# A graph layer on one core: hand-fetched sender rows in every third round instead of every sixth

## The chip, the cores and the metric

The kernel runs on one core of a Trainium2 chip. The metric is device microseconds of one execution, the median of the runs shown. A profile of one execution shows the five engines: PE (TensorE, with its weight loads as PEld), DVE (VectorE), ACT (ScalarE), POOL (GpSimd) and SP (SyncE, which here only starts transfers). Rows named SPq, ACTq and POOLq are instructions that the engine's queue handles itself, such as starting a transfer.

## The reference

One layer of message passing over 12,500 nodes with 128 features and 200,000 edges, sorted by receiver, all in float32:

```python
h = jnp.maximum(_layernorm(x), 0.0)
cat = jnp.concatenate((h[src], h[dst], edge_attr), axis=-1)      # 200000 x 384
msg = jax.nn.relu(cat @ W1 + b1)                                 # 200000 x 128
aggr = jax.ops.segment_sum(msg, dst, num_segments=12500)
t = aggr + h
x = x + gamma * (t - mean(t)) * rsqrt(var(t) + eps) + beta
```

## The kernel before

W1 is split in three. `table_a = h @ W1[0:128]` and `table_b = h @ W1[128:256] + b1` are built per node in DRAM. A message is then a row of `table_a` taken by sender, a row of `table_b` taken by receiver, and the edge's features times the last third of W1.

A **group** is 512 edges: 128 partitions by SUB = 4 edges. There are 391 groups (the last overlaps the one before), UNROLL = 4 of them make a **round**, and there are 98 rounds. Below, (i, u) is group u of round i.

For each group, PE transposes the edge features (`ps_edge`, L756), and ACT copies them out (`edge_cols`, `columns`, L991). DVE writes a one-hot matrix that picks receivers out of a window of 64 rows of `table_b` (`onehot_cols`, `hot_columns`, L1367); SP has loaded that window (`b_win`, `window`, L486) at the group's least receiver, a number that is read into a register. PE makes both products into `ps_pre` (L769, L770). The sender rows come by four gathers on POOL (`a_rows`, L613, in `step`), each an indirect DMA of 128 rows whose numbers DVE wrote a round ahead (`pick`, L1192). DVE adds rows and products (`msg`, `add_a`, L1387), ACT applies the relu (`relu`, L995), PE sums by receiver (`sums`, L781), DVE adds the sums to `aggr` at the group's base (`add_sums`, L1408), which it reads into a register for every group (L1398).

What orders the gathers: `step(i, u)` on POOL waits until `pick` has run for (i, u) and until the add of (i-1, u) has freed `a_rows[:, u]`. So POOL may run four groups ahead of DVE.

Two kinds of work spare POOL gathers. (1) In every sixth round (EARLY = 6), group 3 takes no gather: its `x` rows were gathered at the very start (64 gathers, L588), turned into table rows during the first 64 rounds by a side chain on DVE, PE and ACT (`early_columns` L1007, `keep_early` L1013), stored in `table_early` and loaded by SP in one transfer (`load_early`, L497). (2) In every sixth round (PERIOD = 6) group 0 takes three gathers and not four: the 128 rows of its last quarter are fetched **by hand**, one transfer of 512 bytes per row, 64 rows from SP (`fetch`, L508) and 64 from ACT (`fetch`, L1027). Each fetch loads row numbers from `hand_picks` into registers (L363), 8 at a time on SP, 4 on ACT. SP's are spread over rounds 1 to 4 of the six, ACT's likewise, in the instruction order of their queues. DVE adds the hand rows in an instruction of its own (L1394) behind the add of the other three quarters (L1390).

SP's queue is one list in order. For a round it holds: load four bases; the edges and receivers of groups 0 and 1 (`pair`, L461, L462, which waits for PE and DVE to be done with that half of the round before); windows 0 and 1 (each waits for the products of the same group of the round before, L485); a fetch; the other pair; windows 2 and 3; a fetch; the store of a finished block (L490). The loop on SP and the loop on ACT have a body of six rounds.

ACT's queue in step u of a round: `columns` of the next group; a fetch; in step 3 `deviate` (L973) and `early_columns`; in step 1 `keep_early`; then `relu` of this group.

Of the kernel before, what the change touches and what calls it, by code (L numbers as in the profile page):

```python
# [25 lines left out]
I32 = mybir.dt.int32  # L26
U8 = mybir.dt.uint8
# [4 lines left out]
P = 128  # L32
H = 128
# [14 lines left out]
PERIOD = 6  # L48
BATCH = 8
HAND_K = SUB - 1  # L50
ACT_ROWS = 64
# [7 lines left out]
def build(nc, x, src, dst, edge_attr, w1, b1, gamma, beta, out):  # L59
# [29 lines left out]

    assert HANDS * PERIOD == ROUNDS - 2 and EARLY % PERIOD == 0 and SP_ROWS % BATCH == 0  # L90
    assert PER_GROUP * (UNROLL - 1) + LEAD + WIN <= 3 * P
# [6 lines left out]
    with ctx:  # L98
# [9 lines left out]

        x_all = sb("x_all", [P, ALL_BLOCKS, H])
# [4 lines left out]
        base_i = sb("base_i", [1, ID_ROWS], I32)  # L114
# [13 lines left out]
        flag = sb("flag", [1, 1], I32)  # L128

# [37 lines left out]
        hand_picks = sb("hand_picks", [HANDS, P], I32)  # L167
        hand_rows = sb("hand_rows", [P, 1, H])
# [84 lines left out]
        s_a_rows = [[sem(f"s_a_rows{u}_{k}") for k in range(SUB)] for u in range(UNROLL)]  # L253
# [37 lines left out]
        s_hand_rows = [sem("s_hand_rows")]  # L291
# [12 lines left out]
        s_e_stored = sem("s_e_stored")  # L304
        s_early_loaded = sem("s_early_loaded")
# [43 lines left out]
        def hand_row(p, par):  # L349
            return hand_rows[p:p + 1, par, :].bitcast(U8)  # L350
# [4 lines left out]
        def hand_numbers(t, first, n):  # L355

            if isinstance(t, int):
                return hand_picks[t:t + 1, first:first + n]
            return bass.at_runtime_partition(hand_picks[0:1, first:first + n], t)

        def numbers_of(engine, t, first, n):

            _, numbers = nc.values_load_multi_w_load_instructions(  # L363
                hand_numbers(t, first, n), [engine], min_val=0, max_val=(N - 1) * ROW_BYTES,
                skip_runtime_bounds_check_because="src holds node numbers")
            return numbers
# [14 lines left out]
        def _(sp):  # L381
# [71 lines left out]
            with sp.If(crooked < 1):  # L453
# [18 lines left out]
                def bases(i):  # L472

                    _, values = nc.values_load_multi_w_load_instructions(
                        base_i[0:1, bass.ds(i * UNROLL, UNROLL)], [mybir.EngineType.SP], min_val=0, max_val=N - 1,
                        skip_runtime_bounds_check_because="the least receiver of a group is a node")
                    return values
# [23 lines left out]
                def fetch(t, par, batch):  # L501

                    if batch == 0 and past(t, 1):
                        sp.wait_ge(s_z, ((t - 1) * PERIOD + PERIOD - 1) * UNROLL + 1)
                        sp.sem_inc(s_gate_sp, 1)
                    numbers = numbers_of(mybir.EngineType.SP, t, batch * BATCH, BATCH)
                    for n in range(BATCH):
                        sp.dma_start(hand_row(batch * BATCH + n, par), row_at(numbers[n])  # L508
                                     ).then_inc(s_hand_rows[par], 16)

                def round_(i, t=None, par=None, j=None):
                    base = bases(i)
                    for u in range(UNROLL):
                        if u % PAIR == 0:
                            pair(i, u // PAIR)
                        window(i, u, base[u])
                        if t is not None and (j, u) in SP_SLOTS:
                            fetch(t, par, SP_SLOTS.index((j, u)))
# [3 lines left out]
                def rounds(s):  # L522
                    for j in range(EARLY):
                        n = j // PERIOD
                        round_(s * EARLY + j, s * (EARLY // PERIOD) + n, 0, j % PERIOD)
                    load_early(s)

                SP_SLOTS = [(j, u) for j in range(1, PERIOD - 1) for u in (1, 3)]
                assert len(SP_SLOTS) * BATCH == SP_ROWS
# [5 lines left out]
                rounds(0)  # L535
                with sp.Fori(1, EARLY_GROUPS) as s:
                    rounds(s)
                round_(ROUNDS - 2)
                base = bases(ROUNDS - 1)
                pair(ROUNDS - 1, 0)  # L540
                for u in range(LEFT):
                    if u == PAIR:
                        tail()
                    window(ROUNDS - 1, u, base[u])
# [25 lines left out]
        def _(pool):  # L570
# [35 lines left out]
            with pool.If(crooked < 1):  # L606
                def step(i, u, gathers=SUB):
# [4 lines left out]
                    for k in range(gathers):  # L612
# [3 lines left out]
                        ).then_inc(s_a_rows[u][k], 16)  # L616

                def rounds(s):

                    for n in range(EARLY // PERIOD):  # L620
# [3 lines left out]
                        for u in range(UNROLL if n < EARLY // PERIOD - 1 else UNROLL - 1):  # L624
# [981 lines left out]
```

## Time and profile before

| | us |
|---|---|
| runs shown, lowest to highest | 2840.32 to 2862.66 |
| median of the 3 runs | 2849.47 |
| span of the profiled execution, first to last instruction | 1949.5 |
| median less span: what lies around the instructions | 899.97 |

The profile gives the span of its execution and no device time beside it, so that execution's own time is taken as its span and the 899.97 us that the median has around it. Nothing in the trace shows what these 900 us are. Busy shares are shares of the span; "idle before" is time in which the engine did nothing before an instruction, with what ended the wait. Line numbers are those of the kernel before.

### The profile page before, as it was taken

How to read it: one execution, taken by the hardware profiler on the slowest of the kernel's cores; microseconds unless marked ns; L12 is line 12 of the kernel's file. 1: busy time of each engine (PE TensorE's matmuls, PEld its weight loads, DVE VectorE, ACT ScalarE, POOL GpSimd, SP SyncE). 2: the span in 40 equal slices, each digit the busy share in tenths (PEclk: the TensorE clock that was granted, in tenths of full speed). 3: DMA queues.
4: the chain of work that ended last, by engine and by line, in shares of the span. 5: the costliest groups of instructions: out<-in, count | busy, mean ns of one | idle time of the engine just before them, and what ended most of it. 6: DMA issues, size and time to landing. Idle time of an engine off the chain costs nothing.

```text
span 1949.5 us, 52908 instructions
## 1 busy us (share of the span) xinstructions
PE 1548.5 (79%) x11881; PEld 1483.7 (76%) x11881; DVE 1256.9 (64%) x3454; ACT 659.4 (34%) x1507; POOL 1463.9 (75%) x1559
## 2 busy tenths in 40 slices
PE   5688788778878787877787788787788888877887
PEld 5678788777777777877777787777777877777786
DVE  7656666667666666666666676666566665656665
ACT  5533333333333333333333333333323232322323
POOL 7777777777777777777777777777777777777776
PEclk9888888989889998998989998999898888888988
DMA  9755656556565655656565565656556565555554
GB/s 261 204 143 144 167 143 166 152 156 166 144 169 145 164 152 155 163 147 169 149 160 153 155 166 144 168 140 168 147 154 163 138 164 148 155 148 153 163 145 106
DMA packets 229468, 306.84 MB, mean 157 GB/s; under 512 B 46461, under 2 KB 141157, under 8 KB 229317
## 3 DMA queue, kind: packets, MB, share of 16 engines
q1 hardware_dynamic: 151858, 192.55, 34.4%
q0 software_dynamic: 49536, 101.55, 21.4%
q10 hardware_dynamic: 27922, 11.43, 2.7%
q14 instruction: 143, 1.16, 0.2%
q8 instruction: 9, 0.15, 0.0%
HBM read 281.72 MB, written 23.64 MB: 157 GB/s over the span
## 4 chain that ended last, share of the span: by engine, by line
issue 22%; DMA 22%; POOL 20%; PE 13%; DVE 10%; DVEq 8%; ACT 2%; ACTq 2%; POOLq 1%; SPq 0%
DMA a_rows<-table_a,picks 20%; POOL a_rows L613 19%; DVEq L1398 5%; DVE onehot_cols L1367 3%; PE ps_pre L769 3%; PE ps_pre L770 3%; PE ps_sum L781 2%; DVE msg L1387 2%; PE ps_edge L756 2%; PE ps_fin L781 1%; DVE aggr L1408 1%; ACTq L1027 1%; DMA table_a<-a_out 1%; DVEq L1383 1%; PE ps_sum L788 1%
## 5 line engine op out<-in xcount | busy, mean ns | idle before, releaser
L613 POOL DMA_INDIRECT a_rows<-table_a,picks x1484 | 1401.8, 945 | 452.4 <-issue 400.3
L769 PE MATMUL ps_pre<-w_c,edge_cols 128*128 128x128 f32 x3128 | 671.5, 300 | 29.5 <-issue 29.2
L770 PE MATMUL ps_pre<-b_win,onehot_cols 128*128 128x128 f32 x3128 | 663.2, 297 | 0.0
L995 ACT ACTIVATE msg<-msg 128x512 f32<-128x512 f32 x390 | 245.7, 630 | 951.9 <-DVE msg L1387 893.1
L769 PEld LDWEIGHTS ps_pre<-w_c,edge_cols 128*128 128x128 f32 x3128 | 537.1, 215 | 38.6 <-issue 37.0
L1387 DVE TENSOR_TENSOR msg<-ps_pre,a_rows 128x512 f32<-128x512 f32 x374 | 257.0, 687 | 433.8 <-DMA a_rows<-table_a,picks 339.4
L770 PEld LDWEIGHTS ps_pre<-b_win,onehot_cols 128*128 128x128 f32 x3128 | 534.7, 214 | 0.0
L1367 DVE SCALAR_TENSOR_TENSOR onehot_cols<-space,base_all,ps_hot 64x512 f32<-64x512 int32 x391 | 438.3, 1121 | 0.6 <-DMA space<-in_dst 0.6
L781 PE MATMUL ps_sum<-onehot,msg 128*128 128x64 f32 x1560 | 214.6, 283 | 105.2 <-ACT e_rows L1013 71.3
L781 PEld LDWEIGHTS ps_sum<-onehot,msg 128*128 128x128 f32 x1560 | 200.5, 201 | 123.4 <-ACT e_rows L1013 82.2
L991 ACT ACTIVATE edge_cols<-ps_edge 128x512 f32<-128x512 f32 x391 | 228.4, 584 | 136.8 <-PE ps_edge L756 115.7
L756 PE MATMUL ps_edge<-ident,edges 128*128 128x128 f32 x1564 | 264.9, 297 | 8.4 <-DMA edges<-in_edge_attr 8.4
L781 PE MATMUL ps_fin<-onehot,msg 128*128 128x64 f32 x1560 | 212.2, 283 | 5.6 <-ACT msg L995 5.6
L781 PEld LDWEIGHTS ps_fin<-onehot,msg 128*128 128x128 f32 x1560 | 205.2, 205 | 7.3 <-DVE aggr L1408 6.9
L756 PEld LDWEIGHTS ps_edge<-ident,edges 128*128 128x128 f32 x1564 | 201.6, 162 | 10.5 <-DMA edges<-in_edge_attr 5.9
L1355 DVE TENSOR_TENSOR onehot<-dst_f,ps_hot 128x256 f32<-128x256 f32 x391 | 161.0, 412 | 41.8 <-issue 34.5
L788 PE MATMUL ps_sum<-ident,e_norm 128*128 128x128 f32 x64 | 24.8, 388 | 120.8 <-DVE e_norm L1426 120.8
L788 PEld LDWEIGHTS ps_sum<-ident,e_norm 128*128 128x128 f32 x64 | 10.0, 156 | 129.8 <-DVE e_norm L1426 129.8
L737 PE MATMUL ps_fin<-ident,staged 128*128 128x128 f32 x97 | 29.6, 305 | 79.3 <-DVE aggr L1408 76.0
L1408 DVE TENSOR_TENSOR aggr<-ps_fin,aggr 128x64 f32 x195 | 43.9, 225 | 72.0 <-issue 44.6
L1408 DVE TENSOR_TENSOR aggr<-ps_sum,aggr 128x64 f32 x196 | 43.8, 224 | 65.8 <-PE ps_sum L781 37.9
L737 PEld LDWEIGHTS ps_fin<-ident,staged 128*128 128x128 f32 x97 | 14.4, 149 | 85.4 <-DVE aggr L1408 83.8
(137 smaller groups left out, 1073.8 us busy)
## 6 DMA issues: line engine op xcount, KB each, us to landing
edges<-in_edge_attr SPq DMA_DIRECT2D x195, 512.0 KB
space<-in_dst SPq DMA_DIRECT2D x195, 256.0 KB
a_rows<-table_a,picks POOLq DMA_INDIRECT x1484
hand_rows<-table_a SPq DMA_DIRECT2D x1024, 0.5 KB
hand_rows<-table_a ACTq DMA_DIRECT2D x1024, 0.5 KB
b_win<-table_b SPq DMA_DIRECT2D x391, 32.0 KB
table_b<-b_rows ACTq DMA_DIRECT2D x96, 64.0 KB
out<-out_rows SPq DMA_DIRECT2D x96, 64.0 KB
```

The costliest lines, as they stand in the source:

```text
L613: pool.indirect_dma_start(a_rows[:, u, k, :], None, table_a[:, :], bass.IndirectOffsetOnAxis(ap=picks[:, u, k:k + 1], axis=0),).then_inc(s ...
L756: mm = pe.transpose(ps_edge[u % 2][:, k * P:(k + 1) * P], edges[:, u, k * H:(k + 1) * H], ident[:, :])
L769: pe.matmul(to, edge_cols[:, u % 2, k * P:(k + 1) * P], w_c[:, :], start=True, stop=False)
L770: mm = pe.matmul(to, onehot_cols[:, u % 2, k * P:(k + 1) * P], b_win[:, u, :], start=False, stop=True)
L781: mm = pe.matmul(ps_sums[u % 2], msg[:, u % 2, k, :], onehot[:, u, k, 0:WIN], start=(k == 0), stop=(k == SUB - 1))
L991: act.activation(edge_cols[:, u % 2, :], ps_edge[u % 2][:, :], ACT.Copy).then_inc(s_edge_cols, 1)
L995: act.activation(msg[:, u % 2, :, :], msg[:, u % 2, :, :], ACT.Relu).then_inc(s_msg, 1)
L1355: dve.tensor_tensor(onehot[:, u, :, 0:WIN], dst_f[:, bass.ds(i * UNROLL + u, 1), :].rearrange("p o k -> p (o k)").unsqueeze(2) .to_broadca ...
L1367: dve.scalar_tensor_tensor(out=onehot_cols[0:WIN, u % 2, :].rearrange("w (k p) -> w k p", k=SUB), in0=dst_win[:, u, :].rearrange("w (p k) ...
L1387: dve.tensor_tensor(msg[:, u % 2, :, :].rearrange("p k f -> p (k f)"), ps_pre[u % 2][:, :], a_rows[:, u, :, :].rearrange("p k f -> p (k f) ...
L1398: return dve.value_load(base_i[0:1, bass.ds(g, 1)], min_val=0, max_val=N - 1)
L1408: dve.tensor_tensor(at, ps_sums[u % 2], at, ALU.add).then_inc(s_added, 1)
```

## The change

- PERIOD becomes 3: a quarter of group 0 is fetched by hand in each third round, 32 quarters and no longer 16. POOL does 1468 gathers in the rounds and no longer 1484.
- The split of the 128 rows becomes 72 on SP (nine batches of 8) and 56 on ACT (seven batches of 8, no longer batches of 4). SP has three batches in each round; ACT's lie at steps 0, 2 and 3 of the first two rounds of a period and one at step 2 of the hand round, for the next period.
- `hand_picks` and the bases for SP (`base_sp`) are laid out in places of 16 numbers, so that what one load reads begins on 64 bytes. SP loads 12 bases once for three rounds; DVE loads four once for a round (`base_dve`), and no longer one for each group.
- SP issues the two windows of a half round together, behind one wait for the second group's products; a fetch may lie before the first windows, between windows and pair, between pair and windows, and behind the last windows.
- The loop bodies of SP and ACT hold three rounds; SP's is nested (two of them, then `load_early`), and so are DVE's and POOL's.
- On ACT `early_columns` moves ahead of `columns` in step 3, and the fetch behind `deviate`.
- The four semaphores of the gathers of a group become one; hand rows are waited for by three counts (SP's first five batches, SP's others, ACT's).

```diff
-PERIOD = 6
+PERIOD = 3
 BATCH = 8
+PLACE = 16
-ACT_ROWS = 64
+ACT_ROWS = 56
+FIRST_BATCHES = 5
...
+        def hand_used(t):
+            return ((t - 1) * PERIOD + PERIOD - 1) * UNROLL + 1
...
-                def window(i, u, base):
-                    if u == 0:
+                def windows(i, h, base, end=PAIR):
+                    if h == 0:
                         sp.wait_ge(s_b_stored, 16 if isinstance(i, int) and i < 2 else (i - 1) * 16)
                         sp.sem_inc(s_gate_sp, 1)
                     if past(i, 1):
-                        sp.wait_ge(s_pre, (i - 1) * UNROLL + u + 1)
+                        sp.wait_ge(s_pre, (i - 1) * UNROLL + h * PAIR + end)
                     sp.sem_inc(s_gate_sp, 1)
-                    sp.dma_start(b_win[0:WIN, u, :], table_b[bass.ds(base, WIN), :]).then_inc(s_b_win[u], 16)
+                    for u in range(h * PAIR, h * PAIR + end):
+                        sp.dma_start(b_win[0:WIN, u, :], table_b[bass.ds(base[u], WIN), :]).then_inc(s_b_win[u], 16)
...
+                SLOTS = ((None, 0, 1, 2), (3, 4, 5, None), (6, 7, 8, None))
+                def rounds(t):
+                    base = load_bases(mybir.EngineType.SP, base_sp, t * PLACE, PERIOD * UNROLL)
+                    for j in range(PERIOD):
+                        round_(t * PERIOD + j, base[j * UNROLL:(j + 1) * UNROLL], t, SLOTS[j])
...
+                def round_(i, base, t=None, slots=(None,) * 4):
+                    pair(i, 0)
+                    if slots[0] is not None:
+                        fetch(t, slots[0])
+                    windows(i, 0, base)
+                    if slots[1] is not None:
+                        fetch(t, slots[1])
+                    pair(i, 1)
+                    if slots[2] is not None:
+                        fetch(t, slots[2])
+                    windows(i, 1, base)
+                    if slots[3] is not None:
+                        fetch(t, slots[3])
                     if past(i, 3):
                         store(i - 3)
...
                 with sp.Fori(1, EARLY_GROUPS) as s:
-                    rounds(s)
+                    with sp.Fori(0, 2) as n:
+                        rounds(s * 2 + n)
+                    load_early(s)
...
                     for u in range(groups):
+                        if u == 3 and early:
+                            early_columns(i)
                         if not (last and u == groups - 1):
                             columns(*after(i, u, 1))
-                        if t is not None and j * UNROLL + u < len(ACT_SLOTS) and ACT_SLOTS[j * UNROLL + u]:
-                            fetch(t, par, j * UNROLL + u)
                         if u == 3 and past(i, 2):
                             deviate(i - 2)
-                        if u == 3 and early:
-                            early_columns(i)
+                        for batch in slots[u]:
+                            fetch(t, batch)
...
+                NEXT, SLOTS = ((), (), (0,), ()), (((1,), (), (2,), (3,)), ((4,), (), (5,), (6,)))
...
                 def round_(i, turn, groups=UNROLL, early=False, handed=None, loaded=None):
+                    base = load_bases(mybir.EngineType.DVE, base_dve, i * UNROLL, UNROLL)
...
-                            add_sums(*before(i, u))
+                            add_sums(*before(i, u), base[u])
```

## Rows read from the trace of the kernel before

**Rows 1.** The page: span, and what each engine was busy.

```profile
span 1949.5 us, 52908 instructions
PE 1548.5 (79%) x11881; PEld 1483.7 (76%) x11881; DVE 1256.9 (64%) x3454; ACT 659.4 (34%) x1507; POOL 1463.9 (75%) x1559
```

**Rows 2.** Groups by line on POOL: busy us, mean ns, idle before and its releasers.

```profile
L613 POOL DMA_INDIRECT a_rows<-table_a,picks x1484 | 1401.8, 945 | 452.4 <-issue 400.3 <-DVE picks L1192 52.1
```

**Rows 3.** Waits of POOL: total us, times, longest.

```profile
POOL a_rows L613 <- issue: 400.3, 1313, 0.3
POOL a_rows L613 <- DVE picks L1192: 52.1, 171, 0.3
```

**Rows 4.** Timeline of POOL: the first early gather, the change-over, the last gather.

```profile
5.56 1.10 POOL L588 DMA_INDIRECT aggr<-in_x,early_picks  x1 [3.23 <-DMA early_picks<-in_src]
...
84.39 0.94 POOL L588 DMA_INDIRECT aggr<-in_x,early_picks  x1 [0.30 <-issue]
85.64 0.95 POOL L613 DMA_INDIRECT a_rows<-table_a,picks  x1 [0.30 <-issue]
...
1938.58 0.95 POOL L613 DMA_INDIRECT a_rows<-table_a,picks  x1 [0.30 <-issue]
```

**Rows 5.** Waits of DVE: total us, times, longest.

```profile
DVE msg L1387 <- DMA a_rows<-table_a,picks: 339.4, 154, 5.4
DVE aggr L1408 <- issue: 70.1, 213, 1.2
```

**Rows 6.** Waits of SP's queue: total us, times, longest.

```profile
SPq L485 <- PE ps_pre L770: 350.1, 106, 8.8
SPq L459 <- DVE onehot_cols L1367: 160.7, 73, 8.5
SPq L490 <- DVE out_rows L1340: 87.2, 35, 5.3
```

**Rows 7.** Timeline of SP's queue, one round with two batches and the next one's start.

```profile
799.78 0.41 SPq L461 DMA_DIRECT2D edges<-in_edge_attr  x1
...
801.39 1.26 SPq L486 DMA_DIRECT2D b_win<-table_b  x2
803.38 2.56 SPq L508 DMA_DIRECT2D hand_rows<-table_a  x8
806.21 0.40 SPq L461 DMA_DIRECT2D edges<-in_edge_attr  x1
...
807.64 5.63 SPq L486 DMA_DIRECT2D b_win<-table_b  x2
814.37 2.50 SPq L508 DMA_DIRECT2D hand_rows<-table_a  x8
817.08 0.40 SPq L490 DMA_DIRECT2D out<-out_rows  x1
818.55 0.40 SPq L461 DMA_DIRECT2D edges<-in_edge_attr  x1
```

**Rows 8.** Timeline of SP's queue at the end of its loop's body.

```profile
872.92 0.38 SPq L490 DMA_DIRECT2D out<-out_rows  x1
873.65 0.38 SPq L497 DMA_DIRECT2D a_rows<-table_early  x1
878.00 0.38 SPq L461 DMA_DIRECT2D edges<-in_edge_attr  x1
878.59 0.54 SPq L462 DMA_DIRECT2D space<-in_dst  x1
879.63 1.28 SPq L486 DMA_DIRECT2D b_win<-table_b  x2
881.19 0.39 SPq L461 DMA_DIRECT2D edges<-in_edge_attr  x1
```

**Rows 9.** Timeline of SP's queue and of DVE, the last hand round.

```profile
1880.21 0.41 SPq L461 DMA_DIRECT2D edges<-in_edge_attr  x1
1880.80 0.53 SPq L462 DMA_DIRECT2D space<-in_dst  x1
1881.80 1.27 SPq L486 DMA_DIRECT2D b_win<-table_b  x2
1887.37 0.38 SPq L461 DMA_DIRECT2D edges<-in_edge_attr  x1
...
1896.88 0.54 DVE L1390 TENSOR_TENSOR msg<-ps_pre,a_rows 128x384 f32<-128x384 f32 x1
1897.35 0.27 DVE L1394 TENSOR_TENSOR msg<-ps_pre,hand_rows 128x128 f32<-128x128 f32 x1
```

**Rows 10.** Instructions on the hand rows: ns min/median/max, first and last start.

```profile
L508 SPq DMA_DIRECT2D hand_rows<-table_a x1024: 218/225/328, 93.3 to 1878.0; - x171
L1027 ACTq DMA_DIRECT2D hand_rows<-table_a x1024: 231/235/707, 111.0 to 1891.8; - x171
L1394 DVE TENSOR_TENSOR msg<-ps_pre,hand_rows x16: 268/280/281, 193.1 to 1897.3; 128x128 f32<-128x128 f32 x16
```

**Rows 11.** Timeline of ACT and its queue, step 3 of a round.

```profile
1890.55 1.44 ACTq L1027 DMA_DIRECT2D hand_rows<-table_a  x4
1892.10 0.29 ACT L973 ACTIVATE o_dev<-o_moments,eps 128x1 f32<-128x1 f32 x1 [1.60 <-issue]
1894.18 0.63 ACT L995 ACTIVATE msg<-msg 128x512 f32<-128x512 f32 x1 [1.79 <-DVE msg L1387]
```

**Rows 12.** DMA issues: KB each, us from issue to landing, the shortest two shown.

```profile
table_a<-a_out SPq DMA_DIRECT2D x13, 448.0 KB, 3.9
early_picks<-in_src ACTq DMA_DIRECT2D x1, 4.0 KB, 3.9
```

**Rows 13.** Waits of PE for ACT and for edges: total us, times, longest.

```profile
PE ps_sum L781 <- ACT e_rows L1013: 71.3, 55, 2.6
PE ps_sum L781 <- ACT e_cols L1007: 21.1, 21, 1.2
PE ps_edge L756 <- DMA edges<-in_edge_attr: 8.4, 3, 5.7
PE ps_fin L781 <- ACT msg L995: 5.6, 7, 2.2
PE ps_sum L781 <- ACT msg L995: 3.9, 1, 3.9
```

**Rows 14.** DMA queues: packets, MB, share of 16 engines.

```profile
q10 hardware_dynamic: 27922, 11.43, 2.7%
```

More of the change, by code:

```diff
@@ L499, in load_early, with fetch @@
                                  ).then_inc(s_early_loaded, 16)
-                def fetch(t, par, batch):
+                def fetch(t, batch):
                     if batch == 0 and past(t, 1):
-                        sp.wait_ge(s_z, ((t - 1) * PERIOD + PERIOD - 1) * UNROLL + 1)
+                        sp.wait_ge(s_z, hand_used(t))
                         sp.sem_inc(s_gate_sp, 1)
[L506 to L518, printed above, removed]
+                    numbers = hand_numbers(mybir.EngineType.SP, t, batch)
+                    for p in range(BATCH):
+                        sp.dma_start(hand_row(batch * BATCH + p), row_at(numbers[p])
+                                     ).then_inc(s_hand_sp[0 if batch < FIRST_BATCHES else 1], 16)
@@ L535, in _ @@
                 rounds(0)
+                rounds(1)
+                load_early(0)
                 with sp.Fori(1, EARLY_GROUPS) as s:
-                    rounds(s)
-                round_(ROUNDS - 2)
-                base = bases(ROUNDS - 1)
+                    with sp.Fori(0, 2) as n:
+                        rounds(s * 2 + n)
+                    load_early(s)
+                base = load_bases(mybir.EngineType.SP, base_sp, HANDS * PLACE, 2 * UNROLL)
+                round_(ROUNDS - 2, base[0:UNROLL])
                 pair(ROUNDS - 1, 0)
[L541 to L544, printed above, removed]
+                windows(ROUNDS - 1, 0, base[UNROLL:])
+                tail()
+                windows(ROUNDS - 1, 1, base[UNROLL:], LEFT - PAIR)
                 for b in range(ROUNDS - 4, BLOCKS - 1):
@@ L615, in step, with last_step, hand_round @@
                             bass.IndirectOffsetOnAxis(ap=picks[:, u, k:k + 1], axis=0),
-                        ).then_inc(s_a_rows[u][k], 16)
+                        ).then_inc(s_turn_rows if u == 0 and k == HAND_K else s_a_rows[u], 16)
+                def last_step(i, u):
+                    pool.wait_ge(s_picks, i * UNROLL + u + 1)
+                    pool.wait_ge(s_z, (i - 1) * UNROLL + u + 1)
+                    pool.sem_inc(s_gate_pool, 1)
+                    for k in range(SUB):
+                        pool.indirect_dma_start(
+                            a_rows[:, u, k, :], None, table_a[:, :],
+                            bass.IndirectOffsetOnAxis(ap=picks[:, u, k:k + 1], axis=0),
+                        ).then_inc(s_last_rows[k], 16)
+                def hand_round(i, groups):
+                    for u in range(groups):
+                        step(i, u, HAND_K if u == 0 else SUB)
                 def rounds(s):
-                    for n in range(EARLY // PERIOD):
+                    for n in range(2):
                         with pool.Fori(n * PERIOD, (n + 1) * PERIOD - 1) as j:
@@ L634, in _ @@
                     step(ROUNDS - 2, u)
-                for u in range(LEFT):
+                for u in range(LEFT - 1):
                     step(ROUNDS - 1, u)
+                last_step(ROUNDS - 1, LEFT - 1)
             with pool.Else():
@@ new lines, in hand_round, with rounds @@
+                def hand_round(s, n, early):
+                    loaded = s + n if not isinstance(s, int) or s + n > 0 else None
+                    round_(s * EARLY + n * PERIOD + PERIOD - 1,
+                           (None, s * (EARLY - 1) + n * (PERIOD - 1) + PERIOD), early=early, handed=s * 2 + n + 1,
+                           loaded=loaded)
+                def rounds(s, n, early):
+                    with dve.Fori(0, PERIOD - 1) as j:
+                        plain_round(s, n, j, early)
+                    hand_round(s, n, early)
@@ new lines, in _ @@
+                for j in range(PERIOD - 1):
+                    plain_round(0, 0, j, True)
+                hand_round(0, 0, True)
+                rounds(0, 1, True)
+                half = EARLY_ROWS // EARLY
+                with dve.Fori(1, half) as s:
+                    with dve.Fori(0, 2) as n:
+                        rounds(s, n, True)
+                rounds(half, 0, True)
+                for j in range(PERIOD - 1):
+                    plain_round(half, 1, j, PERIOD + j < EARLY_REST)
```

189 lines of the change are left out of this document (98 added, 91 removed).

## The prediction

> **What bounds the kernel now.** I read the page's busy shares first and saw no answer in them: PE stands highest with 79%, POOL has 75% [rows 1]. The second view is the groups by line. POOL's 1484 gathers take 945 ns each, and before them POOL is idle for 452.4 us, 0.305 us for each one [rows 2]. The third is what those idle times wait for. No single one is longer than 0.3 us, and what ended it is "issue" or the cast that writes row numbers; an add of DVE, which frees a buffer, does not occur [rows 3]. So the gaps are part of a gather and not waits. The timeline shows what that makes: the first gather starts at 5.56 us, the rounds' gathers take over at 85.64 without a gap, and the last starts at 1938.58 [rows 4]. (1938.58 - 85.64) / 1483 = 1.2495 us for one gather with its gap. POOL has one unbroken list from 5.56 to 1939.5, and only 10 us follow. All else is behind it: DVE waits 339.4 us for gathered rows to land [rows 5], and SP's queue waits 350.1 + 160.7 + 87.2 = 598 us, 6.1 us in each of the 98 rounds, for PE and DVE [rows 6]. The page's 75% must not be read as a quarter of slack.
>
> **The term that pays.** 16 gathers go. 16 x 1.2495 = 20.0 us, and since POOL waits for nothing, all of it comes off the end, if POOL goes on waiting for nothing. In three rounds POOL will have 48 gathers less 1 by hand less 2 (the early group, 4 in six rounds) = 45, so 45 x 1.2495 = 56.2 us. That is the time that everybody else has for three rounds.
>
> **SP's queue.** It is the one that may not have it. In the round that starts at 799.78 the next one starts 18.77 us later; two windows took 5.63 us where two without a wait take 1.26, so 4.37 was waiting and 14.40 was work, with two batches of 8 rows [rows 7]. One batch: from the end of the windows (802.65) to the next edges (806.21) is 3.56 us; where no batch lies between, 880.91 to 881.19 is 0.28 [rows 8], so 3.28. The lead into the second batch is 1.10 us, into the first 0.73; the same eight numbers were read, so 0.37 is what I give to where they lie, and the alignment should take it away. A base load: 817.48 to 818.55 is 1.07, less 0.28 is 0.79. A round after: 14.40 + 3.28 - 0.37 - 0.79 = 16.52, three are 49.6. One load of 12 bases was never seen: at least 0.79, at most three of today's, 2.37; I take 1.2, since eight numbers cost at most 1.10 - 0.28 = 0.82. `load_early` adds 873.30 to 874.03 = 0.73 in every second period [rows 8], 0.4 on the mean. Sum 51.2. The end of the loop's body now costs 874.03 to 878.00 = 3.97, less the 1.07 of load and edges, 2.9 us, once in six rounds [rows 8]; after, between nothing and 2.9 in three. So SP works 51.2 to 54.1 us of 56.2. With every bound at its best (a 12-base load of 0.79) it is 50.8; with every one at its worst (2.37 for that load, no gain of 3 x 0.37 by alignment, 2.9 for the loop) 56.4, just past POOL. I take the middle, since the eight-number loads are the nearest rows, and it fits: the third batch lies where SP waits today for PE's products [rows 6]. I cost it at nothing. What hides it is 6.1 us of waiting a round, of which some 1 to 2 stay. With that cover gone each microsecond over 56.2 costs 32 us, one for each period.
>
> The Trainium skill speaks against this: "Runtime: NRT & Kernel Launch", section "Instruction fetch mechanics", says in substance that a register load costs about 200 ns for each register, in bulk too. By that rule eight numbers cost 1.6 us and twelve 2.4, and the sum would be 51.2 + 9 x 1.15 + 1.2 = 62.8 us for three rounds, SP the bound, some 210 us more and 3040 us in all. The rows do not bear it out here: 0.45 us for eight numbers in place [rows 7], so I keep the row's.
>
> **Hand rows in time.** DVE's add of a hand quarter is in order in front of all of DVE's work, so rows that come late stop DVE, and behind it relu, sums and the picks. In the last hand round the pair of edges went out at 1880.21, windows at 1881.80, and the hand add ran at 1897.35 [rows 9]. After, batch 6 comes ahead of those windows, 7 behind them, then a pair (1.3), then 8: 1881.3 + 3.3 + 1.5 + 3.3 + 1.3 + 3.3 = 1894.0 for SP's last row, where today it is 1878.0 [rows 10]. On ACT the last batch starts behind `deviate`, which ended at 1892.39 [rows 11]; lead 0.6 and 2.7 for eight rows (1.44 for four, 0.32 for each further) give 1895.7, today 1891.8 [rows 10]. Landing isn't shown for hand rows: at least 0, at most the 3.9 us of the shortest loads shown [rows 12]. So the last row lands between 1.6 us ahead of the add and 2.2 behind it. I take 1 us late; it costs nothing while POOL is ahead: the buffer freed by this add is next used by the 28th gather from the end, 1938.58 - 27 x 1.2495 = 1904.85, and the add ended at 1897.62. 7.2 us are free here, and 5 more (four gathers) in the hand rounds that no early group follows. DVE's 339.4 us of waiting for gathers [rows 5] take up the rest.
>
> **ACT.** 56 rows in three rounds for 64 in six: 48 more, 48 x 0.32 = 15 us more queue time in six rounds. In step 3 the batch of 8 behind `deviate` puts relu from 1894.18 [rows 11] to about 1895.8, 1.6 us later (2.6 at most, if the lead is long). PE waits for relu 9.5 us in the whole run [rows 13], and reaches the sums only behind the next group's products, so nothing; without that cover 64 such steps of 1.6 us are 100 us of PE and DVE, still not of POOL below 7.2 each. `early_columns` first saves PE at most its 21.1 us of waits [rows 13]; as POOL does not wait for PE, it counts 0 and at the best 0.
>
> **DVE, semaphores, nested loops.** One load of bases a round and not four: at best the 70.1 us of "issue" ahead of L1408 [rows 5], at worst one load's 0.8 us more ahead of a round's first step. Fewer waits in `add_a`. All ahead of work that waits for gathers: 0 on the sum. POOL's own list only loses 16 entries; its branches lie under the gathers today (gap 0.30 throughout [rows 4]), and I bound two more per six rounds by 0 and 0.3 us, 0 to 10 us; I take 0. The 2048 further rows are small packets: 2.7% of 16 engines' span over 27922 packets is 0.030 us each [rows 14], at three packets a row at most 185 us of one engine or 12 of each, which may delay a landing, and POOL doesn't wait for landings; 0, and at most what (b) below costs.
>
> **Sum.** 1949.5 - 20.0 = 1929.5 us of span, and with the 900.0 around it 2829.5, 0.7% less than the median of 2849.47. The runs shown lie 9 below to 13 above that median. About 1% (28.5 us) is what a measurement of this kernel can tell from no change.
>
> **The rivals.** (a) *POOL stays the bound*, the forecast: 2829.5, and 2821 or less if the median falls as low as the lowest run did. For it: not one wait on an add [rows 3]. (b) *Given back*: hand rows come so late that POOL waits. 20.0 us over the 16 hand rounds that an early group follows is 1.25 us each, so the add must be 7.2 + 1.25 = 8.5 us late there; or POOL's branches show. Then 2849. For it: the last rows are due within 2 us of the add; against: 7.2 us are far more than 2.2. (c) *SP becomes the bound*, slower: if its period passes 56.2. Its place is the loop's end, 2.9 us now paid twice as often, with one window wait of 4.37 us kept in a period: 54.1 + 4.4 = 58.5, 2.3 x 32 = 74 us, 2903. For it: 91 to 96% load on a list in order; against: the waits that are left are for work that POOL paces, so they shrink as SP falls behind. The point from which it decides is 5.0 us over my 51.2.
>
> **Chances and range.** (a) 0.78, of which 0.12 lies under 2821, more than 1% faster; (b) 0.12, within 1%; (c) 0.10, slower. So faster 0.12, same 0.78, slower 0.10. The time is (a)'s, 2829.5. The range takes (a) with 13 us of the runs' own scatter below, and (b) with 9 above 2849: 2816 to 2858; (c) is left out.
>
> **What the profile would show.** Right: 1468 gathers at L613's place, no wait of POOL over 0.3 us, pitch 1.25, the last gather some 20 us earlier, SP's waits for products down from 3.6 us a round to 1 or less, hand adds with a wait of 0 to 3 us. Wrong: POOL waiting for DVE's add (b); PE or DVE waiting for windows, edges or receivers and SP waiting for nothing (c); or the 900 us outside the span moving, of which the profile says nothing.

## The result: slower by 6.9%

| | kernel before | changed kernel |
|---|---|---|
| median, lowest to highest, us | 2844.89, 2825.61 to 2862.66 | 3037.14, 3028.14 to 3046.68 |
| ratio, 95% interval | | 1.0687, 1.0629 to 1.0746 |
| its profiled execution: time, span | span 1949.5 | 3033.94, 3032.0 |

The time forecast was 2829.5. One thing must be said before the rows of after are read: the execution of the kernel before whose rows stand ahead of the prediction was unlike the timed ones, and in every timed execution whose span is on record the 900 us that the prediction put around the span lie inside it (shown in e1 below). What the rows of after are set beside in this section is the trace that the prediction was made from; e1 gives the comparison that counts.

The page of the changed kernel, its span, its busy shares and the chain that ended last, to be read beside [rows 1]:

```profile
span 3032.0 us, 55364 instructions
...
PE 1892.5 (62%) x11881; PEld 1788.4 (59%) x11881; DVE 1236.7 (41%) x3473; ACT 658.3 (22%) x1507; POOL 1446.8 (48%) x1543
...
SPq 55%; issue 34%; another core or an unknown queue 4%; PE 4%; DMA 2%; DVE 1%; ACT 0%; DVEq 0%; ACTq 0%
SPq L519 25%; SPq L497 8%; SPq L369 7%; SPq L479 4%; SPq L478 3%; SPq L501 2%; PE ps_pre L804 1%; PE ps_pre L805 1%; SPq L494 1%; DMA edges<-in_edge_attr 1%; SPq L380 1%; SPq L476 1%; SPq L495 1%; SPq L492 1%
```

POOL falls from 75% of its span to 48%, and the chain runs along SP's queue: the hand rows (L519) alone are a quarter of the time. The waits of the changed kernel (us in total, times, longest), POOL's to be read beside [rows 3], SP's beside [rows 6], PE's beside [rows 13]:

```profile
POOL a_rows L632 <- DVE picks L1237: 988.8, 224, 14.4
POOL a_rows L632 <- issue: 489.3, 1236, 11.6
...
SPq L495 <- PE ps_pre L805: 32.9, 5, 7.7
SPq L495 <- remote: 15.0, 6, 5.0
...
PE ps_edge L791 <- DMA edges<-in_edge_attr: 265.7, 75, 11.0
PE ps_pre L804 <- DMA b_win<-table_b: 92.2, 26, 6.8
...
DVE msg L1452 <- DMA hand_rows<-table_a: 68.0, 23, 6.9
```

POOL, which waited for nothing longer than 0.3 us, now waits 989 us for row numbers. SP's 350 us of waiting for products are 48. PE, which waited 8.4 us for edges, waits 266, and 92 for windows: SP brings them late. SP is the bound. Its own instructions on hand rows (ns: least, median, most; first and last start), beside [rows 10]:

```profile
L519 SPq MOVE hand_rows<-table_a x2304: 2/29/1397, 143.6 to 2969.2; - x192
L519 SPq DMA_DIRECT2D hand_rows<-table_a x2304: 2/225/1400, 143.7 to 2969.3; - x192
```

The median of 225 ns is the one of before, but the most is 1400 where it was 328. The timeline of SP's queue says where that lies; the second number is the time from the first instruction of the entry to the end of its last, beside [rows 7]:

```profile
1505.91 6.53 SPq L519 DMA_DIRECT2D hand_rows<-table_a  x8
1512.93 1.14 SPq L497 DMA_DIRECT2D b_win<-table_b  x2
1515.18 4.33 SPq L519 DMA_DIRECT2D hand_rows<-table_a  x8
...
1521.98 2.53 SPq L519 DMA_DIRECT2D hand_rows<-table_a  x8
...
1546.31 2.50 SPq L519 DMA_DIRECT2D hand_rows<-table_a  x8
```

Some batches of eight take the 2.5 us that they took before, others 4.3 or 6.5. Over all 288 batches, from the start of the first row to the start of the last, the mean is 4.10 us, against 2.37 for the 128 of [rows 10].

### The profile page after: what moved, and what is told of

Its sections match the earlier page's. It is cut to its first block, busy times and chain, and to the rows that moved or that the text cites. A ratio compares the mean times of both kernels' runs of the same rounds, so it can differ in the third digit from the quotient of the medians.

```text
span 3032.0 us, 55364 instructions
## 1 busy us (share of the span) xinstructions
PE 1892.5 (62%) x11881; PEld 1788.4 (59%) x11881; DVE 1236.7 (41%) x3473; ACT 658.3 (22%) x1507; POOL 1446.8 (48%) x1543
## 4 chain that ended last, share of the span: by engine, by line
SPq 55%; issue 34%; another core or an unknown queue 4%; PE 4%; DMA 2%; DVE 1%; ACT 0%; DVEq 0%; ACTq 0%
SPq L519 25%; SPq L497 8%; SPq L369 7%; SPq L479 4%; SPq L478 3%; SPq L501 2%; PE ps_pre L804 1%; PE ps_pre L805 1%; SPq L494 1%; DMA edges<-in_edge_attr 1%; SPq L380 1%; SPq L476 1%; SPq L495 1%; SPq L492 1%
## 5 line engine op out<-in xcount | busy, mean ns | idle before, releaser
L804 PE MATMUL ps_pre<-w_c,edge_cols 128*128 128x128 f32 x3128 | 795.2, 344 | 208.1 <-DMA b_win<-table_b 92.2
L805 PE MATMUL ps_pre<-b_win,onehot_cols 128*128 128x128 f32 x3128 | 782.7, 339 | 82.7 <-issue 82.2
L804 PEld LDWEIGHTS ps_pre<-w_c,edge_cols 128*128 128x128 f32 x3128 | 647.0, 255 | 233.9 <-issue 219.8
L805 PEld LDWEIGHTS ps_pre<-b_win,onehot_cols 128*128 128x128 f32 x3128 | 645.4, 254 | 95.2 <-issue 95.1
L791 PE MATMUL ps_edge<-ident,edges 128*128 128x128 f32 x1564 | 310.6, 332 | 297.3 <-DMA edges<-in_edge_attr 265.7
L791 PEld LDWEIGHTS ps_edge<-ident,edges 128*128 128x128 f32 x1564 | 228.2, 180 | 313.1 <-DMA edges<-in_edge_attr 161.4
L816 PE MATMUL ps_sum<-onehot,msg 128*128 128x64 f32 x1560 | 253.5, 316 | 105.8 <-ACT e_rows L1048 48.9
L816 PEld LDWEIGHTS ps_sum<-onehot,msg 128*128 128x128 f32 x1560 | 246.0, 239 | 117.9 <-issue 58.2
L607 POOL DMA_INDIRECT aggr<-in_x,early_picks x64 | 60.5, 946 | 22.5 <-issue 19.2
L1237 DVE CAST picks<-src_f 128x4 int32 (+1 forms) x391 | 64.0, 164 | 0.0
```

The costliest lines, as they stand in the source:

```text
L791: mm = pe.transpose(ps_edge[u % 2][:, k * P:(k + 1) * P], edges[:, u, k * H:(k + 1) * H], ident[:, :])
L804: pe.matmul(to, edge_cols[:, u % 2, k * P:(k + 1) * P], w_c[:, :], start=True, stop=False)
L805: mm = pe.matmul(to, onehot_cols[:, u % 2, k * P:(k + 1) * P], b_win[:, u, :], start=False, stop=True)
L816: mm = pe.matmul(ps_sums[u % 2], msg[:, u % 2, k, :], onehot[:, u, k, 0:WIN], start=(k == 0), stop=(k == SUB - 1))
```

## The experiments

**e1: the kernel before again.** Nothing is edited. The first theory: what slows SP's instructions in the changed kernel is there in the timed executions of the kernel before too. The rival: the change brought it.

> The kernel before, unchanged, to see the execution that the runs time. Theory 1: what made the changed kernel slow (single queue instructions of SP and ACT that take 0.7 us and not 0.03) is there in the timed runs of the kernel before too, and only the profiled execution of before was free of it; then the span here is about 2840 us, within 5 us of the time of the run, SP's queue shows many register instructions of 0.7 us, and POOL waits for DVE. Theory 2: the slow instructions came with the change; then the span is 1950 us again, 900 us below its time, and SP's instructions are as fast as in the trace of before.

Its time was 2858.34 us, and its span is 1.8 us less than that. Page and waits:

```profile
span 2856.5 us, 52908 instructions
...
PE 1855.1 (65%) x11881; PEld 1744.5 (61%) x11881; DVE 1247.8 (44%) x3454; ACT 669.1 (23%) x1507; POOL 1466.5 (51%) x1559
...
another core or an unknown queue 27%; PE 24%; issue 21%; DVE 10%; DVEq 7%; ACTq 4%; SPq 3%; ACT 2%; DMA 1%
```

```profile
POOL a_rows L613 <- DVE picks L1192: 900.3, 237, 12.9
POOL a_rows L613 <- issue: 390.1, 1242, 1.9
...
SPq L485 <- remote: 167.6, 46, 10.6
SPq L485 <- PE ps_pre L770: 80.1, 28, 8.2
...
PE ps_edge L756 <- DMA edges<-in_edge_attr: 51.9, 17, 9.3
...
DVE msg L1387 <- remote: 715.3, 143, 11.1
```

So the first theory held: the change did not bring the slow instructions. It did bring SP into the chain. Set beside e1, POOL's waits for row numbers were there before (900 us, now 989), but SP's share of the chain goes from 3% to 55%, its waits for others in the rounds from some 370 us to 48, PE's waits for edges from 52 us to 266 and those for windows from none to 92.

The 52908 instructions are those of [rows 1], and on POOL, DVE and ACT their own durations too (a gather takes 946 ns; their busy sums are within 2% of [rows 1]). PE is busy 1855 us and not 1548, at a mean granted clock of 0.764 and not 0.899. What is longer besides is the time between instructions. DVE's waits ahead of its add, which in [rows 5] were for rows to land, are now "remote": a semaphore was counted up at a moment at which no instruction in the trace ends. The timeline of POOL, PE, DVE and SP's queue in one stretch shows how:

```profile
1417.14 0.95 POOL L613 DMA_INDIRECT a_rows<-table_a,picks  x1 [5.55 <-DVE picks L1192]
1418.39 0.95 POOL L613 DMA_INDIRECT a_rows<-table_a,picks  x1 [0.30 <-issue]
...
1425.91 0.94 POOL L613 DMA_INDIRECT a_rows<-table_a,picks  x1 [0.30 <-issue]
1430.41 0.94 POOL L613 DMA_INDIRECT a_rows<-table_a,picks  x1 [3.56 <-DVE picks L1192]
...
1419.46 0.39 PE L770 MATMUL ps_pre<-b_win,onehot_cols 128*128 128x128 f32 x2
...
1419.90 1.00 PE L781 MATMUL ps_fin<-onehot,msg 128*128 128x64 f32 x8
1430.34 0.47 PE L788 MATMUL ps_sum<-ident,e_norm 128*128 128x128 f32 x1 [9.44 <-DVE e_norm L1426]
...
1419.28 0.15 DVE L1419 RECIPROCAL e_scale<-e_dev 128x1 f32<-128x1 f32 x1
1428.76 0.69 DVE L1387 TENSOR_TENSOR msg<-ps_pre,a_rows 128x512 f32<-128x512 f32 x1 [9.33 <-remote]
...
1419.36 7.92 SPq L508 DMA_DIRECT2D hand_rows<-table_a  x8
```

The same stretch by windows of 2 us: busy time of PE, PEld, DVE, ACT and POOL, then granted clock, DMA share, GB/s:

```profile
1418.00:1420.00 2.00, 2.00 (x21) 2.00 (x19) 1.43 (x3) 1.10 (x3) 1.38 (x3) 1.00 1.09 294
1420.00:1422.00 2.00, 0.90 (x9) 0.77 (x7) 0.00 (x0) 0.00 (x0) 1.55 (x2) 1.00 0.62 140
1422.00:1424.00 2.00, 0.00 (x0) 0.00 (x0) 0.00 (x0) 0.00 (x0) 1.54 (x2) 1.00 0.22 60
1424.00:1426.00 2.00, 0.00 (x0) 0.00 (x0) 0.00 (x0) 0.00 (x0) 1.39 (x3) 0.54 0.15 40
1426.00:1428.00 2.00, 0.00 (x0) 0.00 (x0) 0.00 (x0) 0.00 (x0) 0.85 (x1) 0.50 0.25 66
1428.00:1430.00 2.00, 0.00 (x0) 0.00 (x0) 0.96 (x4) 0.51 (x1) 0.00 (x0) 0.50 0.13 13
```

POOL has eight gathers to do, two groups, and does them without a pause at 1.25 us each. From 1422 to 1428 PE, DVE and ACT do nothing at all. DVE's add waits for PE's products, and the last product ends at 1419.85 by its record (a modelled end). But the semaphore that it counts up, `s_pre`, moves at 1428.74, 1.9 us after POOL's last gather has ended (1426.85), and within 0.02 us of it the add starts; `s_sum`, for PE's sums that end at 1420.90, moves at 1428.90. The DMA engines are busy only 15 to 25% then, so it is not their bandwidth that is short. SP goes on meanwhile, in steps of 0.7 us, now for a register instruction, now for a transfer: 7.92 us for eight rows. The add lets DVE write the next row numbers, POOL starts on them, and it begins again. In this stretch PE's granted clock falls from 1.00 to 0.50 (2.4 to 1.2 GHz) when PE has stood still. I call this **the hold**.

It is no accident of one stretch. In e1 `s_pre` moves 2.94 us after the end of its products on the mean, over 0.5 us late in 211 of 351 cases, and in 202 of these it moves while POOL pauses, nine times in ten 1.1 to 2.3 us after its last gather. In the trace of [rows 1] the mean is 0.01. The counts of DVE's adds and of ACT's relu come 0.01 us after their ends in the median in both, as far as they are recorded (288 and 277 of 390 in e1). And of SP's 3596 register instructions 553 take 0.6 to 1.5 us where 0.03 is usual: 483 begin while a row of gathers that stand back to back is going on, nearly all behind its first, the other 70 within 1.5 us of such a row's end. In the changed kernel it is 466 and 90 of 556. In the trace of [rows 1] there are none, although POOL never pauses there. So gathers back to back are not enough by themselves: the timed executions differ from that one in something else too, which no run here shows.

So the ring that sets the time in e1 is, by this reading: gathers hold back PE's signal, DVE's add waits for the signal, the row numbers wait for the add, POOL waits for the row numbers, and its wait ends the hold.

**e2 and e3: no hand rows, and hand rows in whole batches.** In e2, from the kernel before, POOL gathers every quarter and nobody fetches hand rows. In e3, from the changed kernel, each batch of eight is one transfer on its queue:

```
-                    for p in range(BATCH):
-                        sp.dma_start(hand_row(batch * BATCH + p), row_at(numbers[p]))
+                    sp.dma_start(hand_rows[batch * BATCH:(batch + 1) * BATCH, :], table_a[0:BATCH, :])
```

> The kernel before with no row fetched by hand: POOL gathers all four quarters of every group but the early ones, 1500 gathers and not 1484, and SP and ACT issue 1024 transfers less each. If POOL sets the end: 16 x 1.25 = 20 us more than before where POOL is unbroken, 1970 us of span. Theory 1 (SP's and ACT's queues set the time in the timed runs, by their number of instructions): far faster than before, between 1970 and 2500 us, as SP's queue has a third less to do. Theory 2 (only the changed kernel has the slow queues): 2870 us, 1% slower than before.

> The changed kernel with each batch of 8 hand rows fetched as one transfer of the first 8 rows of the table, and not as 8 transfers of the rows that the edges name, so the hand rows hold other data; the loads of the row numbers stay. SP issues 288 such transfers and not 2304, ACT 224 and not 1792. If the number of instructions in the queues of SP and ACT makes the time: between 1930 us (POOL's 1468 gathers unbroken) and 2400. If something else in the change does (the nested loops, the paired windows, the order on ACT): about 3037 as the changed kernel.

e2: 2785.72 us, ratio 0.9797 (0.9728 to 0.9866). e3: 2729.3. No expected figure came: e2 lies between its two theories (under 2500, and 2870), and e3 between 2400 and 3037. What they do show is this. In the kernel before hand rows already cost 2846.0 - 2785.7 = 60 us (38 to 77 by the interval) instead of saving 20, and in the changed kernel fetching them one by one, with the loads of their numbers (nothing uses these in e3, and they are not in its trace), costs 3034 - 2729 = 305 us. The change's other parts (loops of three rounds, one load of bases for them, windows in pairs) are all in e3, which is faster than either: by themselves they are not what slows it.

**e6 and e7: one queue at a time.** Two theories are left for the 305 us: SP's queue sets the time, or the time grows with the number of instructions executed (some 17 to 18.5 per us in all kernels so far). e6 makes only SP's batches whole, e7 only ACT's, with the edit of e3.

> The changed kernel with SP's nine batches of eight hand rows as one transfer of table rows 0 to 7 each (SP's hand rows hold other data; ACT's 56 stay single). Theory SP (the issue of SP's hand rows, slowed while POOL gathers, sets the time of the changed kernel): 2730 to 2790 us, near the 2727 of the kernel in which both engines' batches are whole. Theory count (3032 - 2727 = 305 us for 8668 instructions less, so 0.035 us each): about 4900 instructions less, 2860 us.

> The changed kernel with ACT's seven batches of eight hand rows as one transfer of table rows 0 to 7 each (ACT's hand rows hold other data; SP's 72 stay single). Theory SP: SP's queue is as long as before, so 2960 to 3035 us. Theory count: about 3800 instructions less, 2900 us. Theory ACT (ACT's rows are what delays): about 2750 us.

e6: 2825.41 us, e7: 2973.64. The chains, e6 and then e7:

```profile
PE 31%; another core or an unknown queue 23%; issue 21%; DVE 11%; ACTq 8%; DVEq 3%; ACT 2%; DMA 0%; SPq 0%
```

```profile
SPq 51%; issue 33%; PE 6%; another core or an unknown queue 5%; DMA 2%; DVE 2%; ACT 1%; DVEq 0%; ACTq 0%
```

The count would have had e6 at 2860 and e7 at 2900; they moved apart instead. With SP's rows whole, 209 us go, and SP leaves the chain; with ACT's whole, 60, and SP stays. But e6 came out 35 us above what theory SP had given it: against e3 (2729), ACT's single rows cost 96 us once SP is out of the way. The 305 us are mainly SP's, and probably not only SP's. e2, e11 and e12 were run four times, the other experiments once, and the kernel before lies up to 27 us apart in the seven executions beside e1 to e3. SP's 209 us are far outside of that; the 35 us may be scatter, and the 60 and 96 show that ACT's rows cost something rather than how much.

**e4 and e5: a pause on POOL.** Theory held: it is the unbroken row of gathers that holds up the others, so a pause should free them, though it makes the list of POOL longer. From the kernel before, e4 has a memset behind every gather and e5 one behind every group; a count `s_idle` keeps the memsets in order.

```
+                    if past(i * UNROLL + u, 1):
+                        pool.wait_ge(s_idle, (i * UNROLL + u) * SUB)
                     pool.sem_inc(s_gate_pool, 1)
                     for k in range(gathers):
                         pool.indirect_dma_start(a_rows[:, u, k, :], ...)
+                        pool.memset(idle[:, k, :], 0.0).then_inc(s_idle, 1)
```

> The kernel before, with a memset of 128x256 on POOL behind every gather (about 0.3 us; 4 per group, 1564 in all), so that no two gathers stand back to back. In the trace of the kernel before run again, register instructions of SP take some 0.7 us only from the second gather of an unbroken row of them until 1.5 us after its end, and DVE's add waits 5 us longer than its rows need to land. Theory held (unbroken gathers hold up the other engines' queues until POOL pauses): if 0.3 us of pause is enough to let them go, the time falls to about POOL's new bound, 1548 x 1.58 + 60 = 2500 us, and SP's slow instructions, 592 before, fall under 150; if a pause so short is not enough, the time stays at 2830 to 2900 and their number over 450. Theory count (time grows with the number of instructions executed, at some 18 per us): 1564 more instructions, 2930 us. Theory POOL as the bound: 1548 x 0.33 = 510 us more, 3370.

> The kernel before, with one memset of 128x1024 on POOL behind every group's gathers (about 1.0 us; 391 in all). Theory held: rows of four gathers with 1.3 us between them; the queues come free after each, POOL's bound is 391 x (5.0 + 1.0) + 60 = 2410 us, and as the hold lasts up to 1.5 us past the last gather the time falls only part of the way, to 2450 to 2750 us. Theory count: 391 more instructions, 2870 us. Theory POOL as the bound: 391 us more, 3240.

e4: 2558.53 us, e5: 2569.59, where the kernel before ran beside them at 2843.19. The groups by line on POOL, e4 and then e5, beside [rows 2]:

```profile
L622 POOL DMA_INDIRECT a_rows<-table_a,picks x1484 | 1413.6, 953 | 557.8 <-issue 455.5
L626 POOL MEMSET idle<- 128x256 f32 x1484 | 484.3, 326 | 1.1
```

```profile
L622 POOL DMA_INDIRECT a_rows<-table_a,picks x1484 | 1404.7, 947 | 705.7 <-issue 630.2
L626 POOL MEMSET idle<- 128x1024 f32 x375 | 363.4, 969 | 0.2
```

484 us of work were added to POOL and 285 us of time went. Of the 900 us of waiting for row numbers 5.8 are left in e4 and 9.2 in e5: POOL is the bound at last, with its new pitch. The hold is shorter, not gone: `s_pre` comes 1.72 us late on the mean in e4 and 1.21 in e5 (2.94 in e1), and SP's register instructions over 0.4 us are 305, not under 150 as expected (592 in e1). Row numbers are now there before POOL wants them; part of that is that POOL, with its memsets, wants them later, and no run separates the two. Theory count (2930) and POOL as the bound of the kernel before (3370) are both far off.

**e8: the changed kernel with the pause of e4.**

> The changed kernel with a memset of 128x256 on POOL behind every gather, as in e4. If the changed kernel is slower only because its SP queue is held up while gathers stand back to back, and POOL is the bound once they don't, it comes out 16 x 1.58 = 25 us under e4's 2558: 2533 us, with SP waiting over 100 us in all for others. If its SP queue is too long even so (1280 hand rows more on SP at 0.42 us are 540 us, and SP's waits in e4 sum up to about 700 us, so little is left), SP is the bound still: 2600 to 2800 us, SP's waits for others under 100 us. If the slowdown has nothing to do with POOL's unbroken gathers: 3000 us and more.

2570.21 us: neither 2533 nor over 2600. Its chain, and SP's waits for products ahead of its windows:

```profile
issue 33%; SPq 30%; POOL 25%; PE 2%; DMA 1%; DVE 1%; POOLq 1%; another core or an unknown queue 1%; ACTq 0%; DVEq 0%; ACT 0%
```

```profile
SPq L498 <- PE ps_pre L819: 18.0, 5, 6.4
...
SPq L498 <- remote: 2.6, 1, 2.6
```

Of the 192 us that the change costs, the pause leaves 2570 - 2557 = 13, little more than one execution can tell from nothing. What remains of the change is no gain: 16 gathers less should give 25 us here. The likely reason, not shown by a run of its own, is that SP, with some 30 us of waiting left in the rounds, has no room, and shares the chain with POOL.

**e9, e10 and e12: how long a pause.** The edit of e4 with a shorter memset: e9 with 64 columns, e10 and e12 with 128 and 192 in the kernel without hand rows (e2). **e11** is e4's kernel again.

> The kernel before with a shorter pause: a memset of 128x64 (about 0.14 us) behind every gather. Theory held, if so short a pause lets the queues go as well as 0.33 us: POOL is the bound, 1548 x (1.25 + 0.16) + 60 = 2240 us. If a pause has to last longer than this to let them go: 2600 to 2850 us, with picks as the releaser of POOL's waits again and rows of up to eight gathers. Theory count: 2930 us.

> The kernel without hand rows (e2: POOL gathers all four quarters of every group) with a memset of 128x128 (about 0.2 us) behind every gather. Theory held: POOL is the bound, 1564 x (1.25 + 0.22) + 60 = 2360 us, if 0.2 us is pause enough; SP's slow instructions under 150. If the hold is there again: 2500 to 2780 us. By the hand rows' own worth in e1 and e2 (2786 against 2846 us), it should not be slower than the kernel before with a pause of the same length would be.

> The kernel of e10 (no hand rows) with the memset at 128x192 (about 0.27 us) instead of 128x128 (0.22 us measured). Theory held: between 0.22 us (2724 us, held still) and 0.33 us (2558 us, POOL the bound) the hold goes away; if it is gone at 0.27 us, POOL is the bound at 1564 x (1.25 + 0.27) + 100 = 2480 us and POOL's waits for picks are under 50 us; if it needs more than 0.27 us, 2550 to 2700 us with waits for picks over 100 us.

> The kernel of e4 (the kernel before with a memset of 128x256 behind every gather) again, timed in rounds against the kernel before. Theory held: 2545 to 2575 us, a ratio of 0.895 to 0.91. If e4's 2558 was a stray execution: within 1% of the kernel before, 2820 to 2870.

The time from one gather's end to the next one's start within a group is read in POOL's timeline, for instance in e9:

```profile
1503.72 0.95 POOL L622 DMA_INDIRECT a_rows<-table_a,picks  x1 [0.16 <-issue]
1504.67 0.17 POOL L626 MEMSET idle<- 128x64 f32 x1
1505.00 0.95 POOL L622 DMA_INDIRECT a_rows<-table_a,picks  x1 [0.16 <-issue]
```

| kernel | gap in a group, us | `s_pre` late, mean us | POOL waits for picks, us | time, us |
|---|---|---|---|---|
| e1, hand rows | 0.30 | 2.94 | 900.3 | 2858 |
| e9, hand rows | 0.33 | 2.72 | 466.1 | 2812 |
| e4 and e11, hand rows | 0.49 | 1.72 and 1.02 | 5.8 and 10.3 | 2558 and 2556.49 (ratio 0.9049, 0.9001 to 0.9097) |
| e2, none | 0.30 | 2.93 | 796.6 | 2786 |
| e10, none | 0.38 | 2.82 | 265.6 | 2724 |
| e12, none | 0.44 | 2.33 | 2.5 | 2497.36 (ratio 0.8841, 0.8792 to 0.8890) |

In all paused kernels the gap between two groups is at least 0.95 us, since the wait on `s_idle` lets POOL run dry. In e9 and e10 the second of the expected cases came, the hold is there again: 0.03 us more in a group and 0.7 between groups were not enough. In e12 the first came. The time goes with POOL's waits for picks, not with the mean delay of `s_pre`: e4 and e11 are one kernel with one time and differ by 0.7 us in the delay, and e12 has it nearly as long as e9. e12 is the fastest, 11.6% under the kernel before and without the hand rows that the change doubled. That does not price the hand rows: against e11 its 1500 memsets are 0.053 us shorter (80 us) and it has 16 gathers more (25 us at its pitch of 1.56), which alone leaves 55 of the 59 us between them. Its waits on POOL:

```profile
POOL a_rows L620 <- issue: 442.9, 1421, 2.4
POOL a_rows L620 <- POOL idle L624: 60.9, 75, 0.9
```

## Why the prediction was wrong

**What bounds the kernel: the step that failed.** "POOL has one unbroken list", so 16 gathers are worth 20.0 us. That is what [rows 2 to 4] show, of an execution that the timed ones do not resemble. The sign stood in my own table: 900 us "around the instructions", a third of the time, left unexplained and carried through the sum as a constant. In e1 the time around the span is 1.8 us. The Trainium skill has a sentence on this that I did not weigh: "Runtime: NRT & Kernel Launch", section "The ~15µs preamble/postamble breakdown", gives some 6 us as the gap between a profile's total time and the time that the runtime reports, the profile's being the longer. Here it is the device time that is longer than the span, by 1.8 us in e1, so the runs do not bear out its figure; but both are a few microseconds, and 900 us are not. In the timed executions POOL waits 900 us for row numbers, so it is not the bound and 16 gathers less need not come off the end; nor did the 16 that e2 adds show as a cost.

**SP's queue: right queue, wrong size.** This step ("it fits", "I cost it at nothing") is why the change was slower and not merely useless. I had SP working 51.2 to 54.1 us of 56.2. Outside of the stretches with unbroken gathers (taken from the second gather to 1.6 us behind the last) one of SP's instructions takes 0.201 us from start to start in the changed kernel, and a period of three rounds has some 274 of them, so 55 us: the working was nearly right for the conditions of [rows 7 and 8]. Inside those stretches, which are 1924 us of the 3032, it is 0.484. A period took 88.6 us on the mean of 31. So rival (c) named what happened, SP as the bound, PE waiting for windows and edges, SP waiting for nothing, and had its price at 74 us where the change cost 192. Its mechanism was another, too: I looked for it at the loops' ends, and it lies in the rows themselves, 4.10 us a batch and not 2.37, nine times a period 15.6 us, and in all that stands between them. (In e1 the kernel before already takes 5.38 us for a batch, but it has four in three rounds and not nine.) The bound "with every one at its worst" was made of rows that were all read under the same fortunate conditions.

**The rule on register loads.** By the rule of the Trainium skill, "Runtime: NRT & Kernel Launch", section "Instruction fetch mechanics", I had worked out 3040 us, and 3037 was measured. This is a coincidence, not a confirmation:

```profile
L369 SPq TENSOR_LOAD <-hand_picks x288: 3/898/1109, 143.0 to 2966.0; - x144
```

Eight numbers take 0.9 us in the median, held ones included, and not 1.6, and in the chain the loads (L369) have 7% where the rows themselves (L519) have 25%. The sum by the rule put all of the excess into the loads. My own 0.45 us was misread too: it is what was left of a gap after a subtraction, and the 128 such loads of the trace before take 0.53 to 0.98 us, 0.76 in the median. Nor did the alignment take anything away: outside of the hold the loads of the changed kernel take 0.91 in the median. The load of 12 bases, taken at 1.2, measured 0.92.

**ACT at nothing: not borne out.** PE was to hide ACT's 48 further rows per six rounds. ACT's single rows cost 60 us with SP's beside them (e7) and 96 without (e6 against e3). That is for all 1792 of them, in single executions; what the 768 that the change adds cost by themselves no run shows.

**Hand rows in time: right on the mean.** DVE waited 68.0 us in 23 waits for them, 3.0 on the mean, the worst 6.9. I had between nothing and 3. As POOL was not the bound, the 7.2 us of slack that I gave the add played no part.

**Loops, bases, order: right that they cost nothing, as far as shown.** With hand rows in whole batches e3 is 56 us under e2, so together with 32 gathers less they gain, if anything.

## What to carry over

Set the span of a profiled execution against the device time first; if a third is missing, the trace is not of the executions that count, and no sum should be made on it. Price an instruction from an execution of the kind that is timed: a batch of the same eight rows, beside the same gathers, took 2.37 us in one kind and 5.38 in the other. And an engine whose list has no gap need not be the bound: here its rows of gathers went with late signals from the engines that feed it, and giving it more to do made the kernel 10% faster (e11).

## What was not expected of the hardware

- In the timed executions, while POOL has indirect gathers back to back (0.30 us from end to start), the semaphores that PE's matmuls count up move 2.9 us late on the mean and up to 10 (e1), those of DVE and ACT do not as far as they are recorded, and many register instructions on SP take 0.7 us instead of 0.03. It begins with the second gather and ends 1 to 2 us behind the last.
- Gaps of 0.49 us in a group with 1.1 between groups bring the delay to 1.7 us in one execution (e4) and 1.0 in another of the same kernel (e11), gaps of 0.30 with 1.76 between groups to 1.2 (e5); with gaps of 0.33 and 0.38 it is 2.7 and 2.8 (e9, e10).
- The Trainium skill, "SBUF — State Buffer", section "Who interferes with whom", says that "DMA never contends with a compute engine". That is said of SBUF's ports, and no run here shows which path is blocked. The windows of e1 show compute engines standing still while gathers are issued, so the sentence must not be read as saying that gathers cannot hold up other engines; here it came by way of a signal.
- What stays open: what the hold is made of, whether an idle gap of the same length would do as well as a memset, how much of the 900 us is PE's lower clock, and why the execution of [rows 1 to 4] had unbroken gathers and no hold. No run here tells these.
- One rival is untested: that the recording of the profile has a part in the hold. Each timed execution whose span is on record was recorded in some way, none is known to have run without, and e1's trace holds 15,982 semaphore counts where that of [rows 1] holds 50,140 of the same program, so records are lost in it. A plain cost for each recorded instruction is not the answer: e4 has 1935 instructions more than e1 and takes some 285 us less than the kernel before.
